# One-hot comparisons against lane numbers in PSUM, norms in three parts, reused turned tiles and an earlier degree row, in a four-layer graph network

## What is computed

```python
edge_index = jnp.stack([src, dst])
x = _layernorm(x + L0(x, edge_attr, batch0, edge_index, ...))   # h = x@w1.T+b1
#   msg = silu(h[src] + edge_attr@we.T + be); agg = segment_sum(msg, dst)
#   out = silu((1+eps)*h + agg); graph_norm(out + x) over all nodes
x = _layernorm(x + L1(x, edge_index, ...))                      # h = x@W_w+W_b
#   e = leaky_relu(h[src]@a_src + h[dst]@a_dst + a_b)
#   out = segment_sum(softmax(e over all edges) * h[dst], src)
x = _layernorm(x + L2(x, ..., src, dst))                        # Q, K, V, 8 heads of 16
#   score = clip(K[src].Q[dst]/4, -5, 5); softmax of each dst node, times V[src]
x = _layernorm(x + L3(x, edge_attr, src, dst, ...))
#   effect = mlp([x[src], x[dst], edge_attr]); agg = segment_sum(effect, dst)
#   mlp([x, agg])
```

## Time and profile before

| | us |
|---|---|
| median of 3 runs | 5128.94 |
| lowest, highest | 5123.88, 5137.18 |
| the profiled execution | 5134.93 |
| its span, first to last instruction | 5133.1 |
| mean granted PE clock | 0.78 |

### The profile page before, as it was taken

One profiled execution on the slowest core, in us unless ns is written; L12 is line 12 of the kernel. 1 busy time (PEld: TensorE's weight loads), 2 busy tenths in 40 slices (PEclk: granted clock), 3 DMA queues, 4 the chain that ended last, 5 costly groups with the idle time before them and its releaser, 6 DMA issues. The chain is left out here.

```text
span 5133.1 us, 90861 instructions
## 1 busy us (share of the span) xinstructions
PE 3898.4 (76%) x19981; PEld 3483.2 (68%) x19982; DVE 3031.3 (59%) x7847; ACT 1588.7 (31%) x2762; POOL 3431.5 (67%) x3536
## 2 busy tenths in 40 slices
PE   4565656544999999986867566656649999999997
PEld 3555555544988888885756555555548888888884
DVE  6555555567443433436886666666676666666665
ACT  1111111113333333325643222222224444444432
POOL 3777777742777777775426777777744777777760
PEclk7768676665666565668988776777769999999999
DMA  4333333337333333336744444444426666666651
GB/s 121 103 102 103 103 103 103 103 76 114 105 101 104 101 105 101 101 92 164 189 126 146 127 128 125 128 126 127 127 69 183 177 177 177 178 177 177 178 154 32
DMA packets 490869, 645.62 MB, mean 126 GB/s; under 512 B 94487, under 2 KB 354027, under 8 KB 490638
## 3 DMA queue, kind: packets, MB, share of 16 engines
q1 hardware_dynamic: 346174, 312.09, 22.5%
q0 software_dynamic: 132032, 325.99, 22.4%
q10 hardware_dynamic: 12560, 6.52, 1.0%
HBM read 554.44 MB, written 89.82 MB: 126 GB/s over the span
## 5 line engine op out<-in xcount | busy, mean ns | idle before, releaser
L1504 POOL DMA_INDIRECT R<-table_ps,r_idx x832 | 815.6, 980 | 361.3 <-issue 294.0
L1111 POOL DMA_INDIRECT by_src<-R,p_idx x832 | 823.8, 990 | 342.3 <-issue 224.0
L1289 POOL DMA_INDIRECT R<-table_kv,h_idx x832 | 821.0, 987 | 329.9 <-issue 303.6
L606 POOL DMA_INDIRECT R<-table,c_idx x784 | 767.0, 978 | 269.7 <-issue 220.9
L1317 PE MATMUL psum<-R,h_oh 128*128 128x137 f32 x1664 | 371.2, 388 | 390.9 <-DVE R L1430 387.8
L637 PE MATMUL psum<-R,c_oh 128*128 x1664 | 339.9, 368 | 424.8 <-ACT R L647 342.6
L1317 PEld LDWEIGHTS psum<-R,h_oh 128*128 128x128 f32 x1664 | 314.9, 272 | 440.9 <-DVE R L1430 433.3
L637 PEld LDWEIGHTS psum<-R,c_oh 128*128 128x128 f32 x1664 | 287.5, 260 | 475.1 <-issue 475.1
L1634 DVE TENSOR_TENSOR R<-R,psum 128x256 f32 x832 | 347.1, 417 | 394.1 <-PE psum L1536 393.0
L1524 PE MATMUL psum<-w_L_gnn_re_w,r_ea 128*128 128x256 f32 x1664 | 496.4, 380 | 5.5 <-ACT R L1564 5.5
L1525 PE MATMUL psum<-R 128*128 x1664 | 495.8, 380 | 0.0
(11 more groups left out here) (328 smaller groups left out, 7748.8 us busy)
## 6 DMA issues: line engine op xcount, KB each, us to landing
R<-by_src SPq DMA_DIRECT2D x220, 260.0 KB, 3.1
r_ea<-in_ea_t SPq DMA_DIRECT2D x832, 64.0 KB
R<-in_ea_t SPq DMA_DIRECT2D x196, 256.0 KB
R<-rel_rows SPq DMA_DIRECT2D x104, 256.0 KB
R<-lo_rows SPq DMA_DIRECT2D x104, 256.0 KB
h_rel<-rel_rows SPq DMA_DIRECT2D x208, 128.0 KB, 3.3
r_rel<-rel_rows SPq DMA_DIRECT2D x208, 128.0 KB
by_src<-R,p_idx POOLq DMA_INDIRECT x832, 2.4
```

Source lines behind the costliest of these rows:

```text
L606: g.indirect_dma_start(out=rows[:, u, :], out_offset=None, in_=table, in_offset=bass.IndirectOffsetOnAxis(ap=idx[:, j // GROUPS % 2, u:u + ...
L1111: g.indirect_dma_start(out=by_src, out_offset=bass.IndirectOffsetOnAxis(ap=idx[:, u:u + 1], axis=0), in_=rows[:, u, :], in_offset=None).th ...
L1289: g.indirect_dma_start(out=rows[:, u, :], out_offset=None, in_=table, in_offset=bass.IndirectOffsetOnAxis(ap=idx[:, u:u + 1], axis=0)).the ...
L1504: g.indirect_dma_start(out=rows[:, u, :], out_offset=None, in_=table, in_offset=bass.IndirectOffsetOnAxis(ap=idx[:, u:u + 1], axis=0)).the ...
```

## The change

1. In `phase_conv_edges` and `phase_heads` PE writes the lane numbers once into PSUM bank 7 (a product with the identity), and the one-hot comparisons (L684, L1388) read them from there and not from SBUF.
2. In `phase_relation` the one-hot comparison (L1603) is made in two instructions of half the size.
3. `Norm` works in three parts of 12, 20 and 18 tiles. The residual sum ahead of it is made part by part, ACT copies turned chunks between its shares, and DVE adds the bias of the first part's chunks before the last part's result.
4. `Linear` keeps all turned tiles; a second `Linear` on the same X reads them and turns and copies nothing. In heads and relation ACT alone clears the node sums (before, ACT and DVE half each).
5. The degree row is turned and stored in `phase_relation`. `phase_update` only loads it, in three pieces, with a semaphore each.
6. In `phase_place` half of each sum over all nodes is made by PE (seven 512-wide products with ones), the other half by DVE. `Order`'s steps are cut in three: the start in front as before, `find_last` behind the first node sum, `find_places` behind the centring. The wait for the stored step table stands ahead of the norm.
7. `match_high` and `count_high` stop after the 196 groups that have edges; the rest is cleared.

```diff
@@ class Linear
+    def __init__(self, ..., bias, OUT, turned_x, tiles, norm, scale=1.0, per=4, shared=None):
...
         def multiply(n):
-            pe.wait_ge(self.copied, n + 1)
+            at, t = self.chunks[n]
+            if first is None:
+                pe.wait_ge(self.copied, n + 1)
...
-                               self.tile_t[:, n % self.RING, q * P:(q + 1) * P], self.W, start=True, stop=True)
+                               self.turned_x[:, at + q, :], self.W, start=True, stop=True)
...
+        if first is None:
+            unrolled(self.count, turn, multiply, lags=(0, 1))
+        else:
+            unrolled(self.count, multiply, lags=(0,))
@@ class Norm
-    HALVES = (slice(0, NT // 2), slice(NT // 2, NT))
+    CUTS = (slice(0, 12), slice(12, 32), slice(32, NT))
...
-    def __init__(self, nc, c, sem, name, cuts=HALVES, on_vector=(10, 16), room=None):
+    def __init__(self, nc, c, sem, name, cuts=CUTS, on_vector=(4, 6, 10), room=None):
...
+    def vector(self, link, v, Y, OUT, make, linear):
+        for n, cut in enumerate(self.cuts):
+            middle = cut.start + (6 if n else cut.stop - cut.start)
+            make(cut)
+            ins = self.count(v, Y, cut.start, middle)
+            if n:
+                self.finish(link, v, n - 1)
+                self.apply(v, Y, OUT, n - 1)
+                if n >= 2:
+                    linear.vector(v, self.cuts[n - 2].stop)
+                ins = self.count(v, Y, middle, cut.stop)
+            ins.then_inc(self.counted, 1)
+            self.moments(link, v, n)
+        self.finish(link, v, len(self.cuts) - 1)
+        self.apply(v, Y, OUT, len(self.cuts) - 1)
+
+    def scalar(self, a, Y, OUT, linear):
+        ahead = 0
+        for n, cut in enumerate(self.cuts):
+            self.scalar_root(a, n)
+            self.scalar_apply(a, Y, OUT, n)
+            per = linear.chunks[0][1]
+            ahead = cut.stop // per if n == 0 else ahead + 2
+            linear.scalar(a, ahead if n + 1 < len(self.cuts) else None)
@@ phase_conv_edges (phase_heads alike)
+        lane, lane_set = k.psum[:, 7, 0:P], sem("lane_set")
...
+                pe.matmul(lane, k.ident[:], k.lane[:], start=True, stop=True).then_inc(lane_set, 1)
...
-                    v.tensor_tensor(oh[:, j % 2], k.lane[:].unsqueeze(1).to_broadcast([P, G, P]),
+                    v.tensor_tensor(oh[:, j % 2], lane.unsqueeze(1).to_broadcast([P, G, P]),
...
-                staggered(v, PER, (match_high, 0, STEP_GROUPS), ... (count_high, 0, STEP_GROUPS), loads=1)
+                staggered(v, PER, (match_high, 0, TILE_GROUPS), ... (count_high, 0, TILE_GROUPS), loads=1)
@@ phase_place, vector
+                v.wait_ge(made, 2)
                 v.sem_inc(x_used, 1)
...
-                link(v.tensor_reduce(total[:, 0, :], Y.rearrange("p t d -> p d t"), AX.X, ALU.add))
+                link(v.tensor_reduce(total[:, 0, :], Y[:, HALVES[1], :].rearrange("p t d -> p d t"), AX.X, ALU.add))
                 v.sem_inc(want, 1)
+                order.find_last(link, v)
                 v.wait_ge(have, 1)
+                link(v.tensor_reduce(stat[:, 0, :], k.psum[:, 0, :].rearrange("p (q d) -> p d q", d=D), AX.X, ALU.add))
...
+                order.find_places(link, v)
                 v.wait_ge(squared, 2)
...
+                v.wait_ge(order.kept, 16)
+                norm.vector(link, v, Y, k.X[:], scale_and_add, linear)
@@ phase_relation
-        of_target = Linear(..., Dh, tile_t, RT, norm)
+        of_target = Linear(..., Dh, S, RT, norm, shared=of_source)
...
+                sp.wait_ge(deg_copied, 1)
+                sp.dma_start(k.deg_dram, deg_t).then_inc(deg_stored, 16)
...
+                nc.scalar.copy(agg.rearrange("p t w -> p (t w)"), k.none[:].to_broadcast([P, NT * HID])).then_inc(zeroed, 1)
-                v.memset(agg[:, 0:ON_VECTOR, :], 0.0).then_inc(zero, 1)
...
+                    for h in range(2):
+                        ins = v.tensor_tensor(oh[:, j % 2, 2 * h:2 * h + 2], k.lane[:].unsqueeze(1).to_broadcast([P, 2, P]),
+                                              k.rel_cols[:, bass.ds(i * U + G * j + 2 * h, 2)]..., ALU.is_equal)
+                    ins.then_inc(oh_ready, 1)
@@ phase_update
+        pieces = [slice(a * P, b * P) for a, b in ((KEPT, KEPT + 4), (KEPT + 4, RT), (0, KEPT))]
+                for piece, made in zip(pieces, row_made):
+                    sp.dma_start(deg_rows[:, piece], deg_flat[:, piece].to_broadcast(...)).then_inc(made, 16)
-                sp.wait_ge(fold_copied, 1)
-                sp.dma_start(k.deg_dram, deg_t[:]).then_inc(row_made, 16)
-                sp.wait_ge(row_made, 16)
-                sp.dma_start(deg_rows, ....to_broadcast([P, NP])).then_inc(row_made, 16)
...
-                    v.wait_ge(row_made, 32)
+                    v.wait_ge(row_made[2 if at < KEPT else min(n, 1)], 16)
```

More of the change, by code:

```diff
@@ L404, with __init__ @@
     RING = 3
-    def __init__(self, nc, k, sem, name, X, W, cols, bias, OUT, tile_t, tiles, norm, scale=1.0, per=4):
+    def __init__(self, nc, k, sem, name, X, W, cols, bias, OUT, turned_x, tiles, norm, scale=1.0, per=4, shared=None):
         self.nc, self.k, self.X, self.W, self.bias, self.OUT = nc, k, X, W, bias, OUT
-        self.tile_t, self.norm, self.scale, self.cols = tile_t, norm, scale, cols
+        self.turned_x, self.norm, self.scale, self.cols, self.shared = turned_x, norm, scale, cols, shared
+        self.copies = self.sums = 0
         self.chunks = [(at, min(per, tiles - at)) for at in range(0, tiles, per)]
@@ L417, in bank, with tensor @@
         return 2 + self.banks * (n % self.RING) + at // self.fit
-    def tensor(self, pe, after=None):
+    def tensor(self, pe):
+        first = self.shared
         def turn(n):
@@ L954, in _ @@
                 nc.scalar.activation(stat[:, 2, :], stat[:, 1, :], ACT.Sqrt).then_inc(rooted, 1)
-                norm.scalar(a, Y, k.X[:])
-                linear.scalar(a)
+                norm.scalar(a, Y, k.X[:], linear)
+                a.wait_ge(linear.product, linear.count)
                 def distance(i, j):
@@ L1233, in _, with phase_heads @@
                 v.wait_ge(added, PAIRS * (SORTED // G + BANKS))
-def phase_heads(nc, k, attended, Y, KV, table, Q, agg, AW, room, room_t, before):
+def phase_heads(nc, k, attended, Y, KV, table, Q, agg, AW, room, before):
     with ExitStack() as c:
@@ L1295, in _ @@
                 kv.tensor(pe)
-                query.tensor(pe, after=kv)
+                query.tensor(pe)
                 pe.wait_ge(query.added, query.count)
+                pe.matmul(lane, k.ident[:], k.lane[:], start=True, stop=True).then_inc(lane_set, 1)
                 regs = {}
```

215 lines of the change are left out of this document (104 added, 111 removed).

## The result

| | before | after |
|---|---|---|
| median, us | 5131.04 | 5096.52 |
| lowest, highest | 5123.88, 5137.18 | 5094.11, 5099.88 |
| span of the profiled execution | 5133.1 | 5095.2 |

The ratio is 0.9934, with a 95% interval from 0.9922 to 0.9945. The change is faster by 34.5 us where the prediction had 66. The sign was right, the time (5096.5 against 5063) lies half a microsecond above the top of the range.

A forecast was written before the change was run, and what follows sets the result against it. POOL issuing gather behind gather was taken to bound the conv and heads loops, PE the relation loop. Terms -18 - 17 - 3 - 5 - 5 - 13 - 5 = -66 took 5134.9 to 5069, 5063 on the median's scale; range 5040 to 5096.

The forecast's parts named there:

- Lane numbers, conv: Conv loop: PSUM lanes stop L684 stretching gathers, 18 of 20 us gained, bounds 0 to -20.
- Lane numbers, heads: Heads loop: PSUM lanes free L1388's half, by busy time, of 34 us in long gathers; -17, bounds 0 to -34.
- rival B: Heads loop: the hold-ups move to the messages multiply L1411, +22 us, total 5085; chance 0.13.
- Rival A: Comparisons don't hold gathers up, or the moved ones still do; only the stages gain, total 5098; chance 0.08.
- Rival C: Relation loop: PE waits in each group and its clock falls from 1.00; at 10% slow, total 5170; chance 0.03.
- Comparison in two parts: Relation loop: PE hides POOL's gain and DVE's free time covers the extra instruction; 0 us, bounds 0 and +31.
- Node stage of place: Place: node sums halved, POOL's bias starts earlier, SP's queue arrives last; -5 us, bounds -12 and +8.
- Node stage of heads: Heads: five chunks copied early, less added norm work, -3.6 us; with a shorter loop start -5, bounds -9 and +2.
- one stall of the ring (1.6): Node stage of heads: one wait priced at 1.6 us among the costs of the norm in three parts.
- Node stage of relation: Relation: first product -3.6 us, second loses turns 5.7 and PE's wait 3.8; -13, bounds -17 and -5.
- Degree row: Update: loading the row early removes PE's 3.56 us idle and about 1.5 of slow clock; -5, bounds -3 and -7.
- Rival D: Node stages: SP's queue in place and early chunks at low clock swallow the stages' gains, total 5091; chance 0.08.

The follow-up runs named there:

- e8: Changed kernel with PE's node-stage order mended, lanes in PSUM in place and attend loops, head weights in PSUM, relation's comparison whole: 5044.24 us, ratio 0.9833.
- e18: As e17, with the head weights of the heads loop's messages multiply read from PSUM too: 5042.64 us, ratio 0.9828.
- e5: Kernel before with only the lane numbers of the conv and heads comparisons in PSUM: 5106.91 us beside 5130.35, ratio 0.9952.
- e6: Changed kernel with PE multiplying one part's last chunk before turning the next part's first: 5085.79 us beside 5130.35, ratio 0.9911.
- e1: Same kernel as e6, timed where the kernel before took 6424 to 6493 us: ratio 0.9914.
- e13: Kernel before with four inert instructions on DVE at the head of the attend stage: ratio 1.0019.
- e17: Changed kernel with PE's node-stage order mended and lanes in PSUM in the place and attend loops: 5067.71 us, ratio 0.9871.
- e9: Same kernel as e13, timed where the kernel before took 6424 to 6493 us: ratio 0.9999.

## Why the prediction was right or wrong

The mechanism of the largest term was right and the change is faster, but half of the 66 us didn't come. Three steps failed: the split of the heads loop's long gathers by busy time (7.8 us short), the stall on DVE in each node stage, which the sum had as 1.6 us in heads and relation and as nothing in place and which was 4.8 to 6.1 (the three stages together came 15.0 us short, and PE's order mended gave 14.8), and the attend stage and the place loop, which stood at nothing (7.9).

**What bounds the kernel**: right. POOL's gaps stayed at 0.30 us and the two gather loops shortened by what the gathers lost (746.7 against 767.0 us busy, -20.3, and the loop -20.3).

**Lane numbers, conv** (-18): right, -20.3; nothing took over what L684 had held. **Lane numbers, heads** (-17): mis-sized. The gathers' busy time went from 821.0 to 811.8, -9.2. The step that failed is the split by busy time, together with the low chance that I gave rival B because the phase is not free: the comparison's own share was 18.3, near my 17, but 8.9 of it came back on the messages multiply. Of rival B's 22 us 8.9 came true, and e8 and e18, in which the multiply holds nothing, show it. Rival A is out: in e5 the edit alone shortened both loops. Rival C is out: PE's clock in relation stayed at 1.00. The page's rule (the Trainium skill, SBUF — State Buffer, Who interferes with whom), that a tensor_tensor leaves descriptor writing alone, is contradicted by e8's heads loop as well. **Comparison in two parts** (0): right here. **Counting** (-3): right, -3.1.

**Node stage of place** (-5, came -0.1). Up to the scale every step was right, on the old clock 24.25 us later: bias from 1143.0 for 13.99 us, `find_last` held until 1157.0 (7.50 us in a conversion of 50 elements), the wait for the table until 1183.2, the fills from 1184.9 to 1224.6. So far the forecast holds, SP's fills included. SP's queue wasn't last, though: its loads for the loop's first groups were issued by 1228.4, and DVE came to the loop at 1240.4, 9 us later than the 1231 that I gave it. The first scatter follows DVE's first comparison by 13 us in both kernels. The step that failed is DVE's way from the table to the loop. These rows of before and after show it:
```profile
1188.58 6.82 DVE L1016 TENSOR_TENSOR R<-R,p_stat 128x6400 f32<-128x6400 f32 x1
...
1225.80 1.51 DVE L461 TENSOR_TENSOR R<-psum,b_scored 128x390 f32<-128x390 f32 x3
```
```profile
1203.85 1.51 DVE L472 TENSOR_TENSOR R<-psum,b_scored 128x390 f32<-128x390 f32 x3
...
1216.19 0.57 DVE L1090 TENSOR_TENSOR R<-lane,early_cols 128x400 bf16<-128x400 f32 x1
```
DVE began the scale 5.4 us earlier than before. From there to the end of its last share of the norm it took 41.0 us against 33.3, 7.7 more where I had priced the pieces at 2: 4.76 us of standing in front of L472, 2.1 for four bias sums and 0.9 for the third part. Behind the norm came 13 chunks, not 11: 12.2 us against 14.7 with 17. That leaves 0.2 us of the 5.4. PE's order mended takes 2.5 (e6) to 4.6 (e1) of the stage away.

**Node stage of heads** (-3.6 and a shorter start of the loop, -1.4; came +3.0 and -3.6). The first failed by 6.6 us in the term "one stall of the ring (1.6)": the stall was 6.11 us on DVE. I had counted five chunks as taken ahead and hadn't looked at where the product of the third stands in PE's order: behind a turn that needs the second part. With that mended (e6) the stage is -2.7 against before, near my -3.6.

**Node stage of relation** (-13, came -7.3). The first product failed alike: +1.1 to the first gather instead of -3.6, and -5.6 with the order mended. The second half was nearly right: from the first gather to PE's loop 27.6 us before and 19.8 after, -7.8 against my -9.5; ACT's clearing began 6.43 us late, for the stored table, which I had not in the sum.

**Degree row** (-5): nearly right, -4.0. The waits of 11.88 and 3.56 us are gone, and the 16 products behind them take 1.95 us where they took 3.55, so both terms came, 5.2 us together:
```profile
4963.41 5.32 PE L1773 MATMUL psum<-R,w_L_gnn_re_w 128*128 128x512 f32 x12
...
4975.03 1.95 PE L1783 MATMUL psum<-w_out,R 128*128 128x128 f32 x16
```
What I hadn't in the sum is the opening: from the end of the last node sum to PE's first L1773 it is 8.2 us against 7.0 to L1725 before, at a granted clock of 0.58 against 0.75.

**Not in the sum**: attend +5.5 (the place of the loop's code, e13) and the place loop +2.4 (its phase). No row of the trace of before shows the first, since it changes with instructions that come ahead. Rival D's amount (5091) was near the result by luck: SP's queue wasn't last in place, and with PE's order mended the heads stage was within 1 us of the forecast, so the clock of the early chunks can't have cost much there. Counted in spans, the forecast was 5133.1 - 66 = 5067.1 and 5095.2 came, 28.1 more: heads lanes 7.8, place stage 4.9, heads stage 6.6 less 2.2 for the loop's start, relation 5.7, update 1.0, attend and place loop 7.9; less 2.4 that conv and the counting gave beyond the forecast, and 1.3 ahead of the conv loop and behind the heads loop.

## What to carry to other kernels

When a product is fed by a norm in parts, walk PE's own order at each seam between the parts: what stands behind the first instruction that needs the next part, and who waits for that. When one of two instructions that hold a queue is taken away, price the other as taking over part of it, and look for what takes both away. A total that moves by a few microseconds in a stage without an edit can be the loop's jump, or nothing that the edit did: compare the periods within the turn before looking for contention.

## What the runs showed of the hardware

- A gather that starts under a DVE instruction with two operands in SBUF, with 0.15 us or more of it still to run, ends 0.81 to 0.83 us behind that instruction's end (129 gathers of the heads loop before): up to 1492 ns where the bare one takes 946. With one operand in PSUM and 32-bit output there was none of it in 832 gathers (e8, longest 1020); with one operand in PSUM and 16-bit output it stayed (43 scatters, e17). A comparison of one tensor of 16-bit values against one value per lane held 51 scatters in the same loop.
- GpSimd's addition of 14 us held a DVE conversion of 50 elements for 7.5 us, and a two-operand step of 0.29 us for 13.07; sums over one operand ran beside it in their usual 5.66 us. That agrees with the Trainium skill (SBUF — State Buffer, Who interferes with whom: whoever comes first holds the shared pair for its whole instruction, and a reduction never contends).
- A loop's jump on DVE took 0.17 or 0.29 us for the same loop, depending on how many instructions stand ahead of it (before against e9 and e13).
- Where the kernel before took 6424 to 6493 us, the engines stood for up to 10 us in about one group of three: in e9's heads loop DVE stood before L1398 in 67 of 206 groups, for 275 us in all, and before L1390 in 64, for 361. In the group looked at closely PE's results reached the others 8 us late. Its products end at 3531.85, by the profile's modelled ends, and DVE goes on at 3540.22:
```profile
3530.80 1.05 PE L1309 MATMUL psum<-R 128*128 x8
...
3540.22 0.69 DVE L1398 TENSOR_TENSOR R<-psum,R 128x512 f32<-128x512 f32 x1 [4.98 <-DMA R<-lo_rows]
```
The row names a DMA, but both DVE and ACT, which waits for no gather there, left their wait for these products at 3539.97. The granted clock was 0.73 against 0.78 there. Why is open.
